# Two latent cross attentions of a Perceiver: queries stored as split halves with four heads interleaved, scores as three one-pass products

## The reference

```python
q_big = jnp.einsum('bshk,hkq->bshq', q_hk, w_kc_q)
kv_rope = kv_c * cos[None] + _rotate_half(kv_c) * sin[None]
q_r = jnp.einsum('bshq,hqr->bhsr', q_big, W_qr)          # L1x also rotates q_big first
k_r = jnp.einsum('bld,hdr->bhlr', kv_rope, W_kr)
attn = jax.nn.softmax(jnp.einsum('bhsr,bhlr->bhsl', q_r, k_r), axis=-1)
ctx_c = jnp.einsum('bhsl,bld->bhsd', attn, kv_rope)
out = jnp.einsum('bhsd,hkd->bshk', ctx_c, w_kc_kv).reshape(b, s, H * K) @ Wo.T
```

## Time and profile before

| | |
|---|---|
| median of three runs | 2112.19 us (2111.12 to 2112.3) |
| span of the profiled execution (its own time is not listed beside it) | 2106.8 us |
| PE busy over the span | 1996.1 us (95%) |
| DVE, ACT, POOL busy | 1203.5, 898.1, 972.1 us |
| bytes moved by DMA | 226.29 MB, mean 107 GB/s |

### The profile page before, as it was taken

How to read it: one execution, slowest core, us unless ns; L and a number is a source line. 1 busy time by engine, 2 the same in 40 slices (tenths; PEclk the granted TensorE clock), 3 DMA queues, 4 the chain that set the end, 5 groups by cost and what they waited for, 6 DMA issues and landing times. The chain is left out here.

```text
span 2106.8 us, 28714 instructions
## 1 busy us (share of the span) xinstructions
PE 1996.1 (95%) x9018; PEld 1421.9 (67%) x9018; DVE 1203.5 (57%) x2739; ACT 898.1 (43%) x2115; POOL 972.1 (46%) x928
## 2 busy tenths in 40 slices
PE   7989999998999999999998999979978999999997
PEld 6868888776688744666656888767655555555553
DVE  4368998567551022555547899779863443444444
ACT  2356666334422100333335666635524444454542
POOL 1266684211352100676768666476203444555552
PEclk9999999999999999999999999989988999999999
DMA  5421221200311100111222121110345999989887
GB/s 209 150 100 42 58 58 37 82 1 1 120 42 52 35 1 0 52 57 61 70 107 66 43 67 43 66 67 1 110 148 154 312 298 327 210 213 221 209 218 186
DMA packets 103411, 226.29 MB, mean 107 GB/s; under 512 B 14288, under 2 KB 56784, under 8 KB 94768
## 3 DMA queue, kind: packets, MB, share of 16 engines
q1 hardware_dynamic: 80688, 170.85, 24.0%
q0 software_dynamic: 21136, 51.11, 11.9%
q10 hardware_dynamic: 1440, 2.49, 0.3%
HBM read 266.86 MB, written 42.48 MB: 147 GB/s over the span
## 5 line engine op out<-in xcount | busy, mean ns | idle before, releaser
L98 PE MATMUL banks<-L1f_w,L1f_xT 128*128 x760 | 265.1, 492 | 1.9 <-issue 1.3
L2872 POOL DMA_INDIRECT moe_sums<-L1f_y,L1f_row x94 | 149.3, 1589 | 219.5 <-DVE L1f_is_who L2739 162.2
L159 POOL TENSOR_TENSOR rstd<-rstd,power 128x1 f32<-128x1 f32 x48 | 35.4, 738 | 361.1 <-DVE rstd L153 361.1
L98 PEld LDWEIGHTS banks<-L1f_w,L1f_xT 128*128 128x128 f32 x760 | 138.0, 192 | 82.0 <-issue 6.8
L2690 DVE SCALAR_TENSOR_TENSOR L1f_z<-banks,L1f_share,L1f_sg 128x192 f32<-128x192 f32 x95 | 39.7, 418 | 147.8 <-ACT L1f_sg L2623 147.7
L2880 POOL DMA_INDIRECT L1f_xg<-moe_rows,L1f_row x95 | 94.2, 991 | 61.5 <-DVE L1f_spare L2730 24.6
L2623 ACT ACTIVATE L1f_sg<-banks 128x192 f32<-128x192 f32 x95 | 31.4, 331 | 206.9 <-PE banks L98 145.5
L98 PE MATMUL banks<-L0f_down,L0f_z 128*128 128x512 f32 x256 | 111.1, 592 | 1.5 <-DVE L0f_z L2147 1.5
L98 PE MATMUL banks<-L0f_hT_hi,L0f_ug_hi 128*128 128x512 f32 x256 | 100.0, 391 | 0.0
L98 PE MATMUL banks<-L0f_hT_hi,L0f_ug_lo 128*128 128x512 f32 x256 | 99.6, 389 | 0.0
L98 PE MATMUL banks<-L0f_hT_lo,L0f_ug_hi 128*128 128x512 f32 x256 | 99.6, 389 | 0.0
(11 more groups left out here) (425 smaller groups left out, 5672.5 us busy)
## 6 DMA issues: line engine op xcount, KB each, us to landing
L1f_w<-in_experts SPq DMA_DIRECT2D x95, 1280.0 KB
L1f_laid<-moe_counts SPq DMA_DIRECT2D x59, 512.0 KB
w<-in_L1x_heads SPq DMA_DIRECT2D x16, 704.0 KB, 4.1
w<-in_L0x_heads SPq DMA_DIRECT2D x8, 1216.0 KB, 5.7
w<-in_wug SPq DMA_DIRECT2D x8, 1024.0 KB, 4.9
L0x_craw<-in_ctx SPq DMA_DIRECT2D x96, 64.0 KB, 2.9
L1x_craw<-in_ctx SPq DMA_DIRECT2D x96, 64.0 KB, 2.2
w<-in_L0x_out SPq DMA_DIRECT2D x4, 1280.0 KB, 5.5
```

The lines of the kernel that those rows point to most:

```text
L98: ins = pe.e.matmul(out, w, m, start=first and n == 0, stop=last and n == len(pairs) - 1)
L159: pool.e.tensor_tensor(self.rstd[:, i:i + 1], self.rstd[:, i:i + 1], self.power[:, 0:1], ALU.pow).then_inc(self.rstd_set.sem, 1)
L2872: pool.e.indirect_dma_start(self.sums[j % 2][:, :], bass.IndirectOffsetOnAxis(ap=self.row[:, j:j + 1], axis=0), self.y[j % self.NY][:], No ...
```

## The change

- **Layout.** `q[P, 3 tiles, 2 halves, 4 groups, 512]` of type fp32r takes the place of `qT`: three tiles (not four) are held in the chip, every query as a high and a low half, and four heads interleaved, so that the 128 columns of a batch (32 tokens, 4 heads) lie side by side. Tokens of a tile are now batch after batch (host layout and rope tables follow).
- **Queries.** ACT writes every high half, DVE then subtracts and writes every low half, both at a step of four elements, in two pieces when t is 0 (three tiles and one). The other five tiles go through `away_next` and `away_far` to `far`, per four heads: 0.5 MB and twice 1 MB. `away_far` has one buffer, so the next four heads wait for `sent_far`. In L1x `fold_u` moves to another bank and behind `narrow`.
- **Score.** Twelve one-pass products of 256 columns with contiguous weights; the keys are split too (`kT`: ACT the high half and one column `last_key`, DVE `keys_lo`).
- **Contexts** are split from the bank `c_bank`: ACT writes the high half contiguously, DVE's `context_lo` the low half. `split_hi`, `split_lo` and `part_hi` are gone; `project_out` reads its weights at every fourth element (`of_head`).
- **Others.** `weigh` is one operation of 1024 columns; `pT` has one buffer; four key buffers for five; POOL splits the keys ahead of rotating the next ones; `take_back` brings one group (512 KB) after each projected part; in L1x the first context rows are loaded behind the last `send`; in L0x context 2 behind the last `send` and all output weights; L0a's and L1a's copies lose their reordering.

```diff
+        self.q = self.sb("q", [P, self.HELD, 2, GROUPS, BANK], F32R)
+        self.far = sh.nc.dram_tensor(f"{name}_far", (P, 2, NT - self.HELD, GROUPS, BANK), F32, kind="Internal").ap()
...
+    def by_head(self, ap, n):
+        return ap.rearrange("p t (n h) -> p t n h", h=OUT_HEADS)[:, :, :, n]
+    def query_places(self, v, h, t):
+        g, n = h // OUT_HEADS, h % OUT_HEADS
+        if t:
+            return [(self.by_head(self.away_far[:, v], n), 0, BANK)]
+        return [(self.by_head(self.q[:, :, v, g, :], n), 0, self.HELD * P),
+                (self.by_head(self.away_next[:, v:v + 1, :], n), self.HELD * P, BANK)]
+    def keep_query_hi(self, act, h, t, bank):
+        for out, a, b in self.query_places(0, h, t):
+            if t or a:
+                self.place_free(act, h, t)
+            act.e.copy(out, bank[:, a:b].rearrange("p (t n) -> p t n", n=P)).then_inc(self.hi_set.sem, 1)
+    def keep_query_lo(self, dve, h, t, bank, sets):
+        dve.wait_ge(self.hi_set, sets)
+        for (out, a, b), (hi, _, _) in zip(self.query_places(1, h, t), self.query_places(0, h, t)):
+            if t or a:
+                self.place_free(dve, h, t)
+            dve.e.tensor_tensor(out, bank[:, a:b].rearrange("p (t n) -> p t n", n=P), hi, ALU.subtract).then_inc(self.lo_set.sem, 1)
+    def send_far(self, sp, q, sets):
+        self.query_kept(sp, sets)
+        for v in range(2):
+            sp.e.dma_start(self.far[:, v, 1:, q, :], self.away_far[:, v].bitcast(F32)).then_inc(self.sent_far.sem, 16)
+    def of_rows(self, b, v, g):
+        at = b % BPT * P
+        return self.q[:, self.slot(b // BPT), v, g, at:at + P]
+    def of_head(self, i, v, h):
+        return self.q[:, self.slot(i), v, h // OUT_HEADS, h % OUT_HEADS:BANK:OUT_HEADS]
...
     def pool_attention(self, pool):
         for b in range(B + self.LAG_VALUES + BPT):
-            if b + 2 < B:
-                self.rotate_keys(pool, b + 2)
             t = b - self.LAG_TURN
...
+            if b + 2 < B:
+                self.rotate_keys(pool, b + 2)
...
             for r in range(2):
-                ins = pe.e.matmul(bank[:, r * 256:(r + 1) * 256], self.of_batch(b, 8 * g + 4 * r, 4), kt[:, 0:LC * P],
-                                  start=True, stop=True)
+                rows = tuple(self.of_rows(b, v, 2 * half + r) for v in range(2))
+                ins = accumulate(pe, bank[:, r * 256:(r + 1) * 256], parts(rows, cut(self.kT[b % 2], slice(None))))
...
     def mix(self, pe, b):
-        pe.wait_ge(self.ctx_set, b)
+        pe.wait_ge(self.ctx_hi, b)
+        pe.wait_ge(self.ctx_lo, b)
...
-        both = (self.part_hi[o % 2][:], self.part_of(self.ctx_lo, o))
-        accumulate(pe, self.out_bank(i), [p for n in range(4) for p in parts(
-            cut(both, slice(None), slice(n * P, (n + 1) * P)), cut(self.wn, slice(None), 4 * part + n))],
+        heads = range(OUT_HEADS * part, OUT_HEADS * (part + 1))
+        accumulate(pe, self.out_bank(i), [p for h in heads for p in parts(
+            tuple(self.of_head(i, v, h) for v in range(2)), cut(self.wn, slice(None), h))],
...
         for b in range(B + self.LAG_VALUES + BPT):
             o, t = b - self.LAG_VALUES - BPT, b - self.LAG_TURN
-            if 0 <= o < self.LAST or o >= self.LAST + 2:
-                self.split_lo(dve, o)
+            if 0 <= b - self.LAG_VALUES - 1 < B:
+                self.context_lo(dve, b - self.LAG_VALUES - 1)
+            if b + 1 < B:
+                self.keys_lo(dve, b + 1)
             if b < B:
                 self.find_peak(dve, b)
...
+    def context_lo(self, dve, b):
+        dve.wait_ge(self.ctx_hi, b + 1)
+        dve.e.scalar_tensor_tensor(out=self.of_batch(b, 1), in0=self.c_bank.rearrange("p (g n) -> p g n", g=GROUPS),
+                                   scalar=self.last_key[:, b % self.NLAST:b % self.NLAST + 1], in1=self.of_batch(b, 0),
+                                   op0=ALU.add, op1=ALU.subtract).then_inc(self.ctx_lo.sem, 1)
...
-        for r in range(4):
-            dve.e.tensor_scalar(dst[:, r, :], dst[:, r, :], rec[:, r:r + 1], None, ALU.mult).then_inc(self.weighed.sem, 1)
+        dve.e.tensor_tensor(dst[:], dst[:], rec.rearrange("p (r o) -> p r o", o=1).to_broadcast([P, 4, LC * P]),
+                            ALU.mult).then_inc(self.weighed.sem, 1)
...
     def sync(self, sp):
         for h in range(XH):
+            if h >= 7 and h % OUT_HEADS == OUT_HEADS - 1:
+                self.send(sp, h // OUT_HEADS - 1)
             self.head_w[h].load(sp)
...
+        self.send(sp, GROUPS - 1)
+        self.first_context(sp)
+        self.out_w[NSLOT].load(sp)
+        self.sync_attention(sp)
```

More of the change, by code:

```diff
@@ L40 @@
 OUT_HEADS = 4
+GROUPS = XH // OUT_HEADS
 SLOT = 2560
@@ L334, in keys_free, with slot, of_batch, sync_attention @@
+    def slot(self, i):
+        return i % self.HELD
+    def of_rows(self, b, v, g):
+        at = b % BPT * P
+        return self.q[:, self.slot(b // BPT), v, g, at:at + P]
+    def of_batch(self, b, v):
+        at = b % BPT * P
+        return self.q[:, self.slot(b // BPT), v, :, at:at + P]
+    def of_head(self, i, v, h):
+        return self.q[:, self.slot(i), v, h // OUT_HEADS, h % OUT_HEADS:BANK:OUT_HEADS]
     def keys_free(self, eng):
         self.queries_done(eng)
[L338 to L354, removed]
+    def sync_attention(self, sp):
+        for b in range(B + 1):
@@ L467, in score @@
     def score(self, pe, b):
-        kt = self.kvT[b % self.NKT]
-        pe.wait_ge(self.kT_set, b + 1)
-        pe.wait_ge(self.q_back, 16 * (b // BPT - self.HALF + 1))
-        for g in range(2):
-            n = 2 * b + g
+        pe.wait_ge(self.kT_hi, 2 * b + 1)
+        pe.wait_ge(self.kT_lo, b + 1)
+        self.taken_back(pe, b // BPT)
+        for half in range(2):
+            n = 2 * b + half
             bank = self.s_bank[n % 3]
@@ L672, in __init__ @@
         self.qr_hi, self.qr_lo = take("qr_hi", 2 * n), take("qr_lo", 2 * n)
-        self.q0_set, self.q1_set = take("q0_set", 2 * n), take("q1_set", 2 * n)
-        self.queries = [(self.q0_set, 2 * n), (self.q1_set, 2 * n)]
-        self.sent = [take(f"expert_landed{i}", 16 * len(range(i, n, 2))) for i in range(2)]
+        self.query_signals()
         self.head_w = [sh.add_weights(sh.d[f"{name}_heads"][g], self.width, [
@@ L989, in __init__ @@
         self.rest_sin, self.pair_set, self.rest_set = take("rest_sin", n), take("pair_set", n), take("rest_set", n)
[L990 to L992 removed]
+        self.narrowed = take("narrowed", n)
+        self.query_signals()
         self.head_w = [sh.add_weights(sh.d[f"{name}_heads"][h], self.width,
@@ L1066, in tensor @@
                 self.narrow(pe, k - 1)
+            if k < n and k % 2 == 0:
+                self.fold_u(pe, k // 2)
         self.tensor_attention(pe)
@@ L1074, in ask @@
         pe.wait_ge(self.qh_lo, k)
+        if k >= 3 and k % 2:
+            pe.wait_ge(self.u_set, (k - 3) // 2 + 1)
         pe.wait_ge(self.ws_hi, h + 1)
@@ L1313, in __init__ @@
         self.qkv = [q_rows, *([sb(f"{key}{i}", [P, n]) for i in range(3)] for key, n in (("kn", kw), ("vn", vw)))]
-        self.qTb = [sb(f"qTb{i}", [P, AT, P]) for i in range(2)]
-        self.pr = [sb(f"pr{i}", [P, AH, S]) for i in range(2)]
+        late = late or [*pair("qTb", (AT, P)), *pair("pr", (AH, S))]
+        self.qTb, self.pr = late[0:2], late[2:4]
         self.pTb = [sb(f"pTb{i}", [P, AT, P]) for i in range(2)]
```

302 lines of the change are left out of this document (153 added, 149 removed).

## The result

The changed kernel takes **2158.5 us** (2154.7 to 2162.3), 1.0218 of the kernel before (95% interval 1.0205 to 1.0230): 46 us slower, where 2118 was forecast with a range from 2097 to 2132. The profiled execution has a span of 2152.9 us.

A forecast was written before the change was run, and what follows sets the result against it. PE was taken to bound the steady part. Terms -19.3 (steady loops), +13.6 (behind tiles), +3.9 and +2.0 (early loops), +9.0 (starts), -3.6 (ends) sum to +5.6 on the median 2112.19: 2118 us, range 2097 to 2132.

The forecast's parts named there:

- edits at nothing: Edits priced at zero: `send` and `take_back` beside PE, `away_far` with one buffer, `pT` with one buffer.
- the starts: Last query to first key of both attentions: slower copies, low halves and a later first key, +9.0 us (+4 to +13).
- Behind a tile: Loop behind a finished tile: PE waits 0.62 for `context_lo` at the mix, 0.62 for POOL's keys; +13.6 us.
- the rival of POOL being held up: A `weigh` of 1024 columns stops POOL for its whole length, +11.5 in ten loops: 2129 us, chance 0.12.
- Steady loops: PE's loop from score 8 to 31 in both attentions: 0.42 less in each of 46 pitches, -19.3 us.
- The score: PE's score in each loop: twelve one-pass products take 1.53 us instead of 2.05, 0.52 less.
- the projection: PE's projection in each loop: weights read at every fourth element cost 0.10 us, between nothing and 0.22.
- The faster rival: POOL and DVE run faster, so waits behind tiles and early-loop costs fall away: 2098.3 us, chance 0.30.
- the slow score: One-pass score products wait for their weight loads one after the other, 0.82 more a loop: 2142 us, chance 0.06.
- Ends: Last projections of both attentions: `split_lo`'s wait gone, -4.97, strided loads in seven last loops +1.4; together -3.6 us.
- Early loops: Loops 3 to 6: `context_lo` and `keys_lo` lengthen DVE's cycle by 0.96 each, +3.9 us L0x, +2.0 L1x.

The follow-up runs named there:

- Run 2: Kernel before the change with the move of `fold_u` alone (bank of the asks, behind `narrow` at even units): 2126.7 us, 1.0066.
- run 1: Changed kernel with POOL splitting the next head's `wq` right behind its first operation of an odd unit in the L1x queries: 2146.3 us, 1.0164.
- run 8: Changed kernel with heads side by side instead of interleaved, so queries are written and projection weights read contiguously; values not the reference's: 2139.4 us, 1.0131.
- run 16: One of the joined kernels, with `folded_lo` behind `find_peak` from the fourth loop on and L1x's last `narrow` in the bank of the asks: 2105.9 us, 0.9971.
- Run 6: Changed kernel with `weigh` again as four operations with one SBUF operand and a scalar column: 2147.2 us, 1.0168.
- run 4: Changed kernel with POOL's root of a finished tile put behind the rotation of the next keys: 2146.6 us, 1.0157.
- run 3: Changed kernel with DVE's `context_lo` and `keys_lo` ahead of the add to x and the statistics of a finished tile: 2171.6 us, 1.0276.
- run 14: One of the joined kernels, with `folded_lo` behind `find_peak` in the early loops and `weigh` as four operations: 2118.1 us, 1.0035.
- the joined kernels: Changed kernel with early `wq` split, DVE's and POOL's orders behind a tile turned, first keys ahead of `away_far` (2111.0 us, 0.9995), and variants with further edits.

## Why the prediction was wrong

**The failed step** is the list of "edits at nothing": the move of `fold_u`, which the change names, is not in it and has no price in the sum, so the L1x queries stood at nothing. It moved 0.93 us of products out of the place where they covered POOL's split of the next head's weights. Run 2 shows 13.0 us in the stage for that alone (15.0 in the medians), run 1 that an earlier split gives 12 back. I had asked what the new low halves cost PE, and not what stood behind the moved step on POOL. The rest of the stage's 21.3, some 8, comes from the query halves: 4.3 in the same waits (run 8, with contiguous writes, has 16.55 a head and waits of 7.3 instead of 11.6 in all), and about 4 from the copies of the last units (run 16 takes off 3.4), for which 1.54 of the 9.0 of the starts was meant. The other misses come to 19 us: without this stage the time would have been 2137, outside the range as well.

**Behind a tile** the mechanism was right, both waits in the places given, and so was the rival of POOL being held up, which I had kept apart from it: 1.58 beside 0.60. The term was 13.6, measured ten times 1.82, 18.2. Of the 0.58 by which 1.82 exceeds the forecast, 0.51 are the later keys (X + 8.75 for X + 8.24). Run 6 removes the long operations and 0.90 of the 1.82; run 4 leaves the mix's share alone, 0.84. The Trainium skill ("SBUF — State Buffer", "SBUF: two separate sides") says that a VectorE operation with two SBUF inputs, against a GpSimd operation that reads SBUF, holds the port pair which both share for its whole length. The trace agrees: a `weigh` of 1.30 adds 0.98 to the POOL operation that it meets.

**Steady loops**: most pitches went from 7.60 (the 7.64 of the earlier trace rows is one of the longer ones) to 7.23, -16.3 over the 44 pitches of scores 10 to 32, where 0.42 each would be -18.5. The score came as forecast; the projection costs 0.19, not 0.10, the mix 0.08 less. So a load of 310 ns is hidden only in part behind a product of 512 columns; with loads of 192 in run 8 the loop is 0.16 shorter. The faster rival, in which nothing waits behind a tile, is excluded by the waits; so is the slow score, by 1.54.

**Starts**: the mechanism was right and the size short, +14.0 with the first scores against 9.0. In L1x the folds end (1149.16) before POOL has the first key (1149.54): the key decides, 10.0 behind the folds' start where 8.8 was taken. In L0x, 1.7 of the 4.9 is the clock of PE, which was in no term: PE stood still for 3.28 up to 119.88 and then ran the folds at a granted clock of 0.54 (windows, columns as in the earlier trace rows), near the lower level of 1.2 GHz; the earlier trace rows had 7.96 for the same eighteen:

```profile
116.60:119.60 3.00, 0.00 (x1) 0.00 (x0) 2.54 (x4) 2.02 (x2) 0.00 (x0) 1.00 0.36 135
120.00:123.00 3.00, 3.00 (x4) 1.15 (x5) 0.63 (x1) 0.59 (x1) 0.00 (x0) 0.54 0.76 276
```

DVE's low halves cost 1.08, not 0.69; run 8 shows 0.68 for the contiguous form. The Trainium skill ("SBUF — State Buffer", "Specifications (TRN2)") says that each step to a new line of 16 bytes pays a penalty. The trace agrees with that for a step of four float32, and the price was nearer to the 1.24 which I did not take.

**Ends**: here the sign was wrong, +3.2 against -3.6. `split_lo`'s wait is gone, and `context_lo` of the last batch waits behind the add and the statistics instead, 2.66. I had seen that order for the loops behind a tile and not used it for the last one; run 3, which turns it, takes 4.6 off each end.

**Early loops**: the price of a loop, 0.96, was right (0.99), and the size short, +9.2 against 5.9. L1x pays 3.7, not 2.0. And the loop that follows them takes 10.9 where it took 8.25 (the next one 7.24 instead of 7.95): there PE, behind a wait of 1.96, takes 1.91 us for the turned probabilities at a granted clock of 0.50 (181.8 to 183.8), the lower level, instead of 1.03. That the stages behind the attentions became 4.9 faster was not forecast and no run was made on it.

## What to carry to other kernels

A step that is moved is priced twice, by what it costs where it goes and by whose work it covered where it stood: here a move of 0.93 us of products cost 13 us with no instruction added. When a chain crosses two engines behind a finished tile, price their orders together: DVE's alone was slower by 13 us, POOL's alone gave 12, both 23. A change that shortens the busiest engine's loop by 5% made the whole 2.2% slower; with its new waits taken out one by one it ended 0.3% under the kernel before (0.9971).

## What was not expected of the hardware

- A `tensor_tensor` of 1024 columns whose second operand is a broadcast column of four lengthens POOL's operation beside it by 0.98 us. Four `tensor_scalar`s of 256 do not (586 to 655 ns for POOL's operation in run 6), but are lengthened themselves: 1.14 us for the four at the least, up to 3.31 beside POOL's rotation in run 14.
- Writes of VectorE at a step of four float32 take 1077 ns for 512 columns against 681 contiguous (run 8), weight loads 310 against 192.
- After PE had stood still for 3.28 us, its granted clock was 0.54 between 120 and 123, and eighteen folds took 9.66 us instead of 7.96.
- The change's runs spread over 7.6 us and those of the joined kernels over 3 to 12, those of the kernel before over 1.2 in the first measurement and 2 to 8 in later ones.
